# Two channel normalisations: square root on ScalarE and reciprocal on VectorE in place of logarithm and exponential

## What is computed

```python
def _ln(x, g, b, eps=1e-05):
    m = jnp.mean(x, -1, keepdims=True)
    xc = x - m
    v = jnp.mean(xc * xc, -1, keepdims=True)
    return xc * jax.lax.rsqrt(v + eps) * g + b

def _pvm(x, ln_g, ln_b, ...):
    x = x.transpose(0, 2, 3, 1)
    xn = _ln(x, ln_g, ln_b)                 # first normalisation
    branches = jnp.split(xn, 4, axis=3)
    outs = [_ss2d(xi, ...) + skip_scale * xi for xi in branches]
    y = jnp.concatenate(outs, -1)
    y = _ln(y, ln_g, ln_b)                  # second normalisation
    y = y @ proj_W + proj_b
    return y.transpose(0, 3, 1, 2)
```

## Time and profile before

| | us |
|---|---|
| runs, median of 3 | 6276.89 |
| runs, lowest and highest | 6272.69, 6279.28 |
| span of the profiled execution | 6270.2 |
| the two iterations of norm0, from the first load to the barrier's end | 27.0 to 98.9 |
| the two iterations of norm1, from the end of the merge to the barrier's end | 4381.0 to 4450.0 |
| ACT_TABLE_LOAD, each | 1.283 |

### The profile page before, as it was taken

One profiled execution on the slowest core, in us unless ns is written; L12 is line 12 of the kernel. 1 busy time (PEld: TensorE's weight loads), 2 busy tenths in 40 slices (PEclk: granted clock), 3 DMA queues, 4 the chain that ended last, 5 costly groups with the idle time before them and its releaser, 6 DMA issues. The chain is left out here.

```text
span 6270.2 us, 83748 instructions
## 1 busy us (share of the span) xinstructions
PE 5167.0 (82%) x21564; PEld 3423.2 (55%) x21564; DVE 4275.8 (68%) x4244; ACT 3892.7 (62%) x8375; POOL 4196.6 (67%) x2703
## 2 busy tenths in 40 slices
PE   4666389999898898998989999845589999965997
PEld 2333155555555555555555555522358888844776
DVE  2666589999999999999999999956231111143433
ACT  2655488888888888888888888834532222233233
POOL 0566589999999999998999999933014444412343
PEclk8888599999999999999999999977789999975898
DMA  3454477777777777777777777764200000013213
GB/s 94 148 186 181 183 241 250 248 248 247 243 250 239 249 247 244 248 247 238 247 246 247 251 246 249 243 216 164 91 18 0 0 0 0 0 38 107 70 58 128
DMA packets 399686, 1073.56 MB, mean 171 GB/s; under 512 B 51470, under 2 KB 94511, under 8 KB 393600
## 3 DMA queue, kind: packets, MB, share of 16 engines
q1 hardware_dynamic: 384544, 1038.35, 49.7%
q0 software_dynamic: 7584, 20.72, 1.0%
q10 hardware_dynamic: 7104, 9.44, 0.5%
HBM read 883.39 MB, written 184.94 MB: 170 GB/s over the span
## 5 line engine op out<-in xcount | busy, mean ns | idle before, releaser
L918 POOL TENSOR_TENSOR scan_hc<-scan_h,scan_c_rep 128x768 f32<-128x768 f32 x1536 | 2749.4, 1824 | 236.7 <-PE scan_ps_y L749 171.4
L749 PE MATMUL scan_ps_y<-scan_hc,keep_ident 128*128 128x512 f32 (+1 forms) x6144 | 2217.2, 489 | 23.5 <-ACT scan_y L784 23.1
L883 DVE TENSOR_TENSOR_SCAN scan_h<-scan_da,scan_h,scan_ps_p 128x768 f32<-128x768 f32 x896 | 1567.8, 1794 | 0.0
L749 PEld LDWEIGHTS scan_ps_y<-scan_hc,keep_ident 128*128 128x128 f32 x6144 | 1066.6, 190 | 822.5 <-issue 737.6
L801 ACT ACTIVATE scan_warm<-scan_du_t 128x128 f32<-128x128 f32 x4608 | 1423.7, 388 | 40.7 <-PE scan_ps_p L740 35.3
L840 ACT ACTIVATE scan_da<-scan_dd,layer_a_neg 128x768 f32<-128x768 f32 x1344 | 1184.2, 921 | 2.2 <-issue 1.6
L1260 POOL TENSOR_TENSOR attn_e_lo<-attn_e,attn_e_hi 128x512 fp32r<-128x512 f32 x324 | 417.6, 1289 | 771.4 <-DVE attn_e_hi L1251 771.4
L740 PE MATMUL scan_ps_p<-keep_ident,scan_warm 128*128 128x128 f32 x4608 | 645.9, 277 | 221.9 <-DVE scan_h L883 221.1
L883 DVE TENSOR_TENSOR_SCAN scan_h<-scan_da,scan_ps_p 128x768 f32<-128x768 f32 x448 | 758.4, 1734 | 2.1 <-ACT scan_da L840 2.0
L740 PEld LDWEIGHTS scan_ps_p<-keep_ident,scan_warm 128*128 128x128 f32 x4608 | 531.5, 142 | 371.8 <-issue 160.4
L862 DVE TENSOR_TENSOR scan_ps_p<-scan_ps_p,scan_dd 128x768 f32<-128x768 f32 x576 | 546.6, 949 | 185.9 <-PE scan_ps_p L732 185.0
(11 more groups left out here) (291 smaller groups left out, 7109.4 us busy)
## 6 DMA issues: line engine op xcount, KB each, us to landing
scan_c_rep<-bc_dram SPq DMA_DIRECT2D x1536, 384.0 KB, 4.1
scan_dd<-dd_dram SPq DMA_DIRECT2D x96, 768.0 KB, 5.6
scan_b_rep<-bc_dram SPq DMA_DIRECT2D x192, 384.0 KB, 4.7
dd_dram<-delta_de SPq DMA_DIRECT2D x96, 384.0 KB, 6.5
dd_dram<-delta_du SPq DMA_DIRECT2D x96, 384.0 KB, 15.7
y_dram<-scan_y SPq DMA_DIRECT2D x96, 384.0 KB, 4.5
merge_y<-y_dram SPq DMA_DIRECT2D x32, 1152.0 KB, 10.3
delta_img<-xn_dram SPq DMA_DIRECT2D x16, 576.0 KB, 10.1
```

The lines of the kernel that those rows point to most:

```text
L749: mm = pe.matmul(ps_y[:, lo:hi], keep["ident"][:, :], hc[t % HR][:, lo:hi], start=n == 0, stop=n == N - 1)
L883: dve.tensor_tensor_scan(view(h[n]), view(x), view(y), start, ALU.mult, ALU.add).then_inc(scan_done, 1)
L918: pool.tensor_tensor(hc[t % HR][:, :], h[t % N][:, :], c_rep[t % CR][:, :], ALU.mult).then_inc(hc_done, 1)
```

## The change

Step 6 becomes sd = Sqrt(var + eps) on ScalarE, and step 7 becomes rs = 1/sd on VectorE. The count of the semaphores stays at eight a tile and iteration; only the engine that adds the seventh is another. Both calls of `norm_phase` are changed, the normalisations in the merge, projection and blend phases are not. Lines of the changed kernel are up to 3 higher than those of the kernel before.

```diff
@@ -247,6 +247,9 @@
                     mean = ps_m[:, ln, 0:TT].unsqueeze(1).to_broadcast([128, 2, TT])
                     dve.tensor_tensor(xc[:, ln, :, :], x[:, ln, :, :], mean, ALU.subtract).then_inc(link[ln], 1)
                 for ln in range(LN):
+                    dve.wait_ge(link[ln], i * STEP + 6)
+                    dve.reciprocal(rs[:, ln, :], sd[:, ln, :]).then_inc(link[ln], 1)
+                for ln in range(LN):
                     dve.wait_ge(link[ln], i * STEP + 7)
                     inv = rs[:, ln, :].unsqueeze(1).to_broadcast([128, 2, TT])
                     dve.tensor_tensor(xc[:, ln, :, :], xc[:, ln, :, :], inv, ALU.mult).then_inc(link[ln], 1)
@@ -260,10 +263,7 @@
                     act.activation(sq[:, ln, :, :], xc[:, ln, :, :], ACT.Square).then_inc(link[ln], 1)
                 for ln in range(LN):
                     act.wait_ge(link[ln], i * STEP + 5)
-                    act.activation(sd[:, ln, :], ps_v[:, ln, 0:TT], ACT.Ln, bias=keep["eps"][:, 0:1]).then_inc(link[ln], 1)
-                for ln in range(LN):
-                    act.wait_ge(link[ln], i * STEP + 6)
-                    act.activation(rs[:, ln, :], sd[:, ln, :], ACT.Exp, scale=-0.5).then_inc(link[ln], 1)
+                    act.activation(sd[:, ln, :], ps_v[:, ln, 0:TT], ACT.Sqrt, bias=keep["eps"][:, 0:1]).then_inc(link[ln], 1)
                 for ln in range(LN):
                     act.wait_ge(link[ln], i * STEP + 8)
                     for h in range(2):
```

## The result

| | median, us | runs | ratio to before, with 95% interval |
|---|---|---|---|
| before | 6277.69 | 6 | |
| changed | 6308.58 | 6 | 1.0048 [1.0032, 1.0064] |

The kernel became slower by 0.48%, about 30 us with an interval from 20 to 40. The forecast was 6307.5, and the mechanism is the one forecast: the reciprocal.

The account below looks back on a forecast made before the run. The bound was norm_phase's chain of hand-overs, with no engine saturated. Reciprocals, less the removed Exp and its load, add 7.65 us an iteration, +30.6 us over four; other terms nothing: 6276.9 + 30.6 = 6307.5 us, range 6292 to 6329.

Parts of the forecast that it names:

- The bound and the one-for-one passage: In norm_phase no engine is saturated; a chain of hand-overs sets the end, so any delay of Identity goes fully into the time.
- The cover by TensorE: In norm_phase TensorE's variances, 7.90 us long, pace ScalarE, so Sqrt in Ln's place costs nothing.
- The price of the reciprocal: Six 128x384 reciprocals on VectorE ahead of the first multiplication, 2570 ns each, lengthen an iteration by 7.65 us.
- The choice of six passes: Reciprocal's estimated 6.4 ns an element against an ordinary pass's 1.05 ns; taken as six passes, 6.3 ns.
- R: Duration of one 128x384 reciprocal on VectorE, taken as 2.57 us; an iteration grows by 6R - 7.77 us.
- Rival B: Reciprocal on VectorE longer still: eight passes, 3.30 us each, an iteration 12.0 us longer, total 6325 us; chance 0.19.
- rival C: Reciprocal's excess on VectorE is only start-up: 0.74 us each, Identity 2.03 us earlier, total 6268.8 us; chance 0.13.
- What goes: Exp and its exposed table load leave ScalarE, freeing 1.28 + 2.59 us and taking 50.08 to 53.97 out of the chain.
- The table loads: New 1.28 us loads ahead of Square and in the projection hide and cost nothing, at most 5.1 us for each place.
- TensorE's clock: TensorE rests 7.65 us longer before the next loads arrive; taken as no cost, up to 4.4 us put into the range.

## Why the prediction was right

**The bound and the one-for-one passage** held. The loss is in the four places where VectorE was idle for 9.23 us, the start of Identity moved, and the doubled reciprocal showed that each microsecond there arrives in the time. The cover by TensorE was read rightly too: the last Sqrt ended 5.18 us behind the first one's start, as Ln had.

**The price of the reciprocal.** Forecast 2570 ns, measured 2552 for the first of six and 2495 for the others. The choice of six passes by the ratio 6.1 was right: 6.25 ns an element, where I had 6.3. That R could be worked out from one small tile was a bet, and the prediction said so: its two rows of one size could not tell six passes from eight.

The mis-sized term is the R of the five reciprocals that stand behind another one: 2.495 us, not 2.57. The overlap of 0.08 us at each seam was right, so the pitch is 2.42 ((14.61 - 2.50) / 5) where I had 2.49. With the first one's 2.552 that accounts for 0.41 us an iteration. Another 0.15 is the way from the first multiplication to Identity: 0.93 us (59.89 to 60.82) where I took 1.08. Identity came 16.07 us behind the first Sqrt, not 16.64. So the loss was 7.08 us an iteration where 7.65 were forecast, 28.3 in all where 30.6 were; by the stages it was 26.9 to 28.3 in the pairs of profiles. The 26.9 of the first pair holds a second thing that no term of the sum has: TensorE's means and what follows up to the first Sqrt were 2.2 us quicker over the four iterations in that profile, and the first matmul came 0.7 us later behind its loads. The median moved by 30.9 us, closer to the forecast than these terms deserve: its interval is 20 us wide, so that this agreement is luck.

The range had a slip that didn't matter: R = 1.9 gives 6291.4, and with the spread of 3 us below it the lower end would be 6288, not 6292.

**Rival B**, eight passes, would have shown 3.3 us, and rival C, a price that is all start-up, 0.74. Both are excluded by the rows of the two sizes. The two statements of the Trainium skill that I set beside them, as I read them there, do not hold here: the repeat count of 8 (VectorE: DVE Perf Modes, "First, the fixed hardware budget") is not the number of passes that an element costs, and one element a cycle (Vector Engine (DVE) Microarchitecture Reference, "Measured stream behaviour on trn2") doesn't hold for the reciprocal. Its 6.25 ns are 6.0 of the ordinary passes of 1.05 ns.

**What goes.** With a copy for the reciprocal Identity starts 2.51 us earlier in an iteration. Rival C's working had 2.03, with 0.74 us for the operation; with the copy's 0.36 it gives 2.41, and the way from the first multiplication to Identity, 0.98 us (50.35 to 51.33) where 1.08 was taken, gives the rest. The saving from Exp and its exposed table load is real, and smaller than what came in.

**The table loads.** The total was right, and the detail was not. I called the gap behind the first Square in norm0's second iteration (2.06 us) the smallest of the four. It is not: in norm1's first iteration, before the change, it is 1.66 us from Square to Square, less than the 2.12 of load and Square:

```profile
4389.02 0.84 ACT L260 ACTIVATE norm_sq<-norm_xc 128x768 f32<-128x768 f32 x1 [16.95 <-DVE norm_xc L248]
4390.68 0.84 ACT L260 ACTIVATE norm_sq<-norm_xc 128x768 f32<-128x768 f32 x1 [0.81 <-DVE norm_xc L248]
```

So the second Square had to be touched there. In the first profile of the changed kernel it was touched in all four iterations. In norm0's first one it runs right behind the first (1.58 us for two), and it is the third that catches up with VectorE, at 38.73 after 0.44 us of idleness. TensorE's first pass was quicker here, so the second subtraction came 2.11 us behind the first in place of 2.56. In norm0's second iteration and in norm1 three Squares run in a row:

```profile
4416.28 1.28 ACT L263 ACT_TABLE_LOAD   x1 [16.65 <-DVE norm_xc L248]
4416.54 0.95 DVE L248 TENSOR_TENSOR norm_xc<-norm_x,norm_ps_m 128x768 f32<-128x768 f32 x1 [0.36 <-PE norm_ps_m L234]
4417.57 2.31 ACT L263 ACTIVATE norm_sq<-norm_xc 128x768 f32<-128x768 f32 x3
...
4420.11 0.84 ACT L263 ACTIVATE norm_sq<-norm_xc 128x768 f32<-128x768 f32 x1 [0.23 <-DVE norm_xc L248]
```

The cover is the six tiles' rhythm of 1.29 us against Square's 0.84, not the first gap alone: each Square behind the first wins back 0.45 us. It held in all four iterations. In the projection the margin was thin too, 0.17 us, where ScalarE waits for the second tile's products:

```profile
4501.29 1.28 ACT L1137 ACT_TABLE_LOAD   x1 [12.21 <-PE proj_ps_x L1111]
4502.58 1.05 ACT L1137 ACTIVATE proj_x<-proj_ps_x,keep_proj_b 128x384 f32<-128x384 f32 x2
4503.80 1.05 ACT L1137 ACTIVATE proj_x<-proj_ps_x,keep_proj_b 128x384 f32<-128x384 f32 x2 [0.17 <-PE proj_ps_x L1111]
```

The third tile's first Identity comes 5.1 to 5.3 us behind the point where the first one could have started, with the load and without it. From the projection's first load to the first Exp of the attention it took 185.8 and 185.5 us in the two profiles of the kernel before, and 187.2, 185.1 and 187.3 in the three of the changed one. The seven variants, which all have these four loads too, took 185.3 to 186.1. So the 1.5 us of two profiles don't go with the loads, and I have no cause for them. The load's 1.28 us with the next activation 0.01 to 0.02 us behind it is again all that a switch costs in the rows.

**TensorE's clock.** I had put up to 4.4 us for longer rests into the range. The rests of the second iterations grew from 16.85 and 16.27 us to 24.20 and 23.63, and the first passes behind them took 9.61 and 9.50 us where they had taken 10.24 and 9.97; in the other profiles of both kernels they took 9.60 to 9.96 after and 9.75 and 9.99 before. So this longer rest cost nothing that can be seen. My reading of the earlier trace rows, that the pass gets longer with the rest ahead of it, doesn't hold in general either. Two of the longest passes of second iterations:

```profile
89.05 10.99 PE L234 MATMUL norm_ps_m<-norm_x,keep_ones_c 128*128 128x384 f32 x24 [38.42 <-DMA norm_x<-in_x]
4416.14 10.95 PE L234 MATMUL norm_ps_m<-norm_x,keep_ones_c 128*128 128x384 f32 x24 [13.87 <-DMA norm_x<-z_dram]
```

The first is of the doubled reciprocal, the second, with a third of the rest, of the copy; in that same profile a pass behind a rest of 14.40 us took 9.42. What sets the length is how long the lower of the clock's two levels (1.2 and 2.4 GHz) lasts at the pass's start: in these second iterations the granted clock is 0.50 there and 1.00 later, and over the whole pass 0.72 and 0.73 in these two, 0.83 in the one of 9.61 us. What decides when it rises, no run here shows.

## What to carry to other kernels

Before a function is moved to another engine, find its price by the element at two sizes: one row of a small tile hides whether it is start-up or slope. Comparing it with an ordinary instruction of the same kind gave the right slope here, but only the second size shows it. VectorE's reciprocal in f32 has a slope six times that of an ordinary pass, so it pays only where the tile is small or the engine has that much rest behind the input: here it broke even at 192 elements for each of six tiles. And when an edit is worth half a per cent, compare the lengths of the stages that it touches, since a long stretch elsewhere can vary by as much as the effect.

## What the runs showed of the hardware

- A reciprocal in f32 on VectorE takes 6.25 ns an element on each partition: 378 ns at 36, 1295 or 1354 at 192, 2495 or 2552 at 384 elements, the longer one where no reciprocal stands right ahead. A copy of 128x384 in its place took 360 ns.
- Its fixed part is 153 ns alone and 95 ns behind another reciprocal; between multiplications it pays nearly the larger (2547 ns on average, tile by tile).
- In a row of equal VectorE instructions that don't need each other's result the next starts 0.08 us ahead of the end of the last; an instruction that needs it starts 0.03 or 0.04 us behind that end.
- ScalarE's function for the reciprocal square root ran at the same 0.58 us for 128x384 as Ln and Sqrt do, so the whole factor costs one pass of ScalarE.
